# A transformer block with a fast-weight layer and a mixture of experts: the set-up reordered, and the narrow products placed on column groups of the array

## The chip, the cores and the metric

The program runs on one core of one Trainium2 chip. Its time is device microseconds (us) for one execution. Five engines run side by side and meet through semaphores: TensorE (PE, the 128x128 matrix array, whose weight loads are listed as PEld), VectorE (DVE), ScalarE (ACT), GpSimd (POOL) and SyncE (SP), which here only issues transfers. Each engine works through its own list strictly in the order written. In the profile a line such as L1412 is line 1412 of the kernel before.

## What is computed

The input `x` is 2048 rows of 512. One vector `c` gives six modulation rows of 512 (`mod = silu(c) @ wmod`, called here row 0 to row 5): shift, scale and gate for the attention half (0, 1, 2) and for the expert half (3, 4, 5).

```
h = layernorm(x) * (1 + row1) + row0
x = x + gate(row2) * fast_weight_layer(h)
h = layernorm(x) * (1 + row4) + row3
x = x + gate(row5) * experts(h)
```

The fast-weight layer has 4 heads of width 128 and walks over 16 chunks of 128 tokens. For each chunk it makes q, k, v (`silu(h @ W_qkv)`, q and k normalised) and 12 learning rates per token (`softplus(h @ W_lr + b_lr)`). It computes gradients for three 128x128 weight matrices per head, passes each through two Newton-Schulz steps in bf16, adds it to the matrix, rescales the columns, and applies the new matrices to q. The next chunk starts from the new matrices, so the 16 chunks are a recurrence. The expert half sends each token to 2 of 8 experts by router logits `h @ (gate_weight.T + 2 * lora)` and adds low-rank terms to the expert weights.

## The kernel before, in words

**Set-up.** All of it stands ahead of the chunk loop in each engine's list. SP issues `c`, rows 1 and 0 of `wmod`, `W_qkv` in four parts by contraction index, row 2, `W_proj`, rows 4, 3, 5 and two chunks of `x`. ACT issues fifteen more transfers (two chunks of `x`, the three fast-weight matrices, `W_lr`, `b_lr`, the router's and the low-rank factors) and only then runs `silu(c)` (L1333), since the transfers stand first in its list. PE makes rows 1 and 0 as columns (L294, L300: 16 products each of one column), turns the three matrices (`turned`, L112), prepares chunk 0 (L322 to L345: twelve products of 512 columns for q, k, v, and four of 12 columns for the rates, L330), and has the other rows between them: row 2 as a broadcast (L340, cbc, with `c` spread over 128 columns), row 4 as columns (L350), row 3 (L360), row 5 (L366). The low-rank term of the first three expert weight tiles (L394, "mg") closes it. From rows 2 and 5 DVE makes the gates (L770 to L778 and L805 to L812).

**Chunk loop.** One iteration `c` interleaves four strands by an order that is written out for each engine: the fast-weight step of chunk `c` (FWD, N0, N1, N2), the preparation of chunk `c+1` (PREP and RATE), the output of chunk `c-1` (APPLY: products with q, projection, layernorm, router logits, ranks, scatter by an indirect transfer from POOL), and three expert weight tiles (MG: L592 adds the low-rank term, DVE scales it, SP stores it in DRAM). The `heads` helper (L106) runs four products of 128 columns, `turned` (L112) four transposes. The rates are four accumulating products of 12 columns (L474) into `P0[:, 0:12]`, the logits four of 8 columns (L578) into `A0[:, 0:8]`. ACT's `sg` (L1412), the first silu of the fast-weight step, marks each chunk once.

**Tail and experts.** After the loop comes the output of chunk 15, a table of expert blocks, and 39 blocks of expert work (L660, L673). The expert weights are read back into the space of the loop's buffers: five experts when iteration 15 begins, three when its updates have been read.

## Time and profile before

| what | value |
|---|---|
| median of 3 runs | 1042.41 us (1042.32 to 1044.21) |
| the profiled execution | 1043.71 us, span 1042.0 us |
| mean granted TensorE clock | 0.945 |
| busy, share of the span | PE 87%, DVE 63%, ACT 61%, POOL 31% |
| chain that ended last | PE 56%, DVE 20%, ACT 12%, issue 5%, POOL 3% |

### The profile page before, as it was taken

How to read it: one execution, taken by the hardware profiler on the slowest of the kernel's cores; microseconds unless marked ns; L12 is line 12 of the kernel's file. 1: busy time of each engine (PE TensorE's matmuls, PEld its weight loads, DVE VectorE, ACT ScalarE, POOL GpSimd, SP SyncE). 2: the span in 40 equal slices, each digit the busy share in tenths (PEclk: the TensorE clock that was granted, in tenths of full speed). 3: DMA queues.
4: the chain of work that ended last, by engine and by line, in shares of the span. 5: the costliest groups of instructions: out<-in, count | busy, mean ns of one | idle time of the engine just before them, and what ended most of it. 6: DMA issues, size and time to landing. Idle time of an engine off the chain costs nothing.

```text
span 1042.0 us, 16297 instructions
## 1 busy us (share of the span) xinstructions
PE 907.1 (87%) x5123; PEld 575.7 (55%) x5123; DVE 654.5 (63%) x2293; ACT 635.7 (61%) x1378; POOL 320.6 (31%) x283
## 2 busy tenths in 40 slices
PE   1798799999999999999999999986539999999995
PEld 1665476577576576575665765764324444444442
DVE  1145889988889889889789899796332222222221
ACT  0114888888888889788888888886113333333331
POOL 0111333433343443343434344332201222222222
PEclk9978999998999999999999999996659999999998
DMA  9603154364362551561652542439523444444430
GB/s 345 227 1 108 35 143 125 80 163 112 92 163 77 127 163 57 137 162 32 163 136 69 162 126 69 133 90 367 211 71 71 75 81 82 78 78 72 82 55 0
DMA packets 58084, 120.43 MB, mean 116 GB/s; under 512 B 6912, under 2 KB 8576, under 8 KB 56976
## 3 DMA queue, kind: packets, MB, share of 16 engines
q1 hardware_dynamic: 45968, 100.23, 32.6%
q0 software_dynamic: 8176, 16.85, 9.9%
q10 hardware_dynamic: 3856, 2.31, 0.7%
q8 instruction: 42, 0.69, 0.3%
q14 instruction: 42, 0.34, 0.1%
HBM read 51.94 MB, written 69.27 MB: 116 GB/s over the span
## 4 chain that ended last, share of the span: by engine, by line
PE 56%; DVE 20%; ACT 12%; issue 5%; POOL 3%; ACTq 2%; DMA 1%; SPq 0%; POOLq 0%; DVEq 0%
PE bank L660 14%; PE bank L106 11%; PE bank L112 7%; PE bank L673 6%; DVE t_small L993 1%; ACT t_arena L1502 1%; PE bank L494 1%; PE bank L480 1%; PE bank L487 1%; PE bank L474 1%; PE bank L464 1%; POOL t_small L1711 1%; POOL xs_scratch L1722 1%; PE bank L456 1%; PE bank L459 1%
## 5 line engine op out<-in xcount | busy, mean ns | idle before, releaser
L106 PEld LDWEIGHTS bank<-t_arena 128*128 128x128 bf16 (+1 forms) x1536 | 120.1, 123 | 99.7 <-ACT t_arena L1518 18.0
L660 PE MATMUL bank<-t_arena 128*128 x312 | 145.8, 610 | 18.9 <-issue 15.0
L106 PE MATMUL bank<-t_arena 128*128 128x128 bf16 (+1 forms) x1536 | 148.5, 237 | 14.4 <-ACT t_arena L1518 5.3
L1748 POOL DMA_INDIRECT out_x<-t_arena,t_tokx x39 | 60.6, 1553 | 208.3 <-DVE t_small L1302 196.9
L112 PE MATMUL bank<-t_ident,t_arena 128*128 128x128 f32 x618 | 97.5, 281 | 22.7 <-DMA t_arena<-xs_scratch 8.3
L112 PEld LDWEIGHTS bank<-t_ident,t_arena 128*128 128x128 f32 x618 | 75.7, 146 | 74.6 <-issue 43.5
L1307 DVE TENSOR_TENSOR t_arena<-t_arena,bank 128x256 f32<-128x256 f32 x39 | 16.4, 422 | 144.8 <-ACT t_arena L1636 144.8
L1636 ACT ACTIVATE t_arena<-bank 128x256 f32<-128x256 f32 x39 | 15.0, 384 | 148.6 <-PE bank L660 148.6
L660 PEld LDWEIGHTS bank<-t_arena 128*128 128x128 f32 x312 | 56.7, 192 | 85.1 <-issue 85.1
L673 PE MATMUL bank<-t_arena 128*128 x156 | 73.5, 593 | 0.5 <-ACT t_arena L1631 0.5
L1643 ACT ACTIVATE t_arena<-bank,t_small 128x128 f32<-128x128 f32 x156 | 58.7, 456 | 16.5 <-PE bank L112 14.5
L1703 POOL TENSOR_TENSOR t_small<-t_small,t_half 128x8 f32<-128x8 f32 x15 | 26.9, 1794 | 115.9 <-DVE t_small L993 115.9
L1313 DVE SCALAR_TENSOR_TENSOR t_arena<-bank,t_small,t_gbb 128x512 f32<-128x512 f32 x39 | 29.3, 751 | 51.7 <-PE bank L673 47.7
L106 PE MATMUL bank<-t_W,t_arena 128*128 128x128 f32 x384 | 55.1, 299 | 1.5 <-DVE t_arena L1181 1.5
L106 PEld LDWEIGHTS bank<-t_W,t_arena 128*128 128x128 f32 x384 | 51.5, 213 | 3.2 <-DVE t_arena L1181 1.7
L112 PEld LDWEIGHTS bank<-t_identb,t_arena 128*128 128x128 bf16 x384 | 27.6, 99 | 39.4 <-issue 18.5
L1722 POOL DMA_INDIRECT xs_scratch<-t_arena,t_posu x30 | 30.3, 1010 | 45.0 <-DVE t_cum L1175 40.4
L112 PE MATMUL bank<-t_identb,t_arena 128*128 128x128 bf16 x384 | 38.0, 222 | 2.7 <-DVE t_arena L878 0.9
L1697 POOL TENSOR_TENSOR t_small<-t_euler,t_small 128x12 f32<-128x12 f32 x15 | 38.3, 2555 | 0.0
L673 PEld LDWEIGHTS bank<-t_arena 128*128 128x128 f32 x156 | 26.7, 190 | 19.9 <-issue 19.9
L112 PE MATMUL bank<-t_ident,t_WT 128*128 128x128 f32 x192 | 35.4, 334 | 0.9 <-DVE t_WT L1141 0.5
L592 PE MATMUL bank<-t_arena 32*128 32x512 f32 x90 | 19.3, 714 | 16.1 <-ACT t_arena L1563 16.1
(489 smaller groups left out, 2220.6 us busy)
## 6 DMA issues: line engine op xcount, KB each, us to landing
xs_scratch<-t_zero SPq DMA_DIRECT2D x16, 2064.0 KB, 15.0
wm_scratch<-t_arena SPq DMA_DIRECT2D x48, 256.0 KB
t_arena<-wm_scratch SPq DMA_DIRECT2D x8, 1536.0 KB, 18.6
t_arena<-xs_scratch SPq DMA_DIRECT2D x39, 258.0 KB, 2.7
t_arena<-in_gate_up SPq DMA_DIRECT2D x32, 256.0 KB, 12.1
t_arena<-in_wmod SPq DMA_DIRECT2D x6, 1024.0 KB, 17.8
out_x<-t_arena SPq DMA_DIRECT2D x16, 256.0 KB, 2.0
t_arena<-in_down SPq DMA_DIRECT2D x16, 256.0 KB, 12.4
```

Of the source, the lines that this page charges most:

```text
L106: mm = pe.matmul(bank[:, s], lhs[:, s], rhs[:, s], start=True, stop=True)
L112: mm = pe.transpose(bank[:, 128 * k:128 * k + 128], src[:, 128 * k:128 * k + 128], idn)
L592: mm = pe.matmul([P0, P1, P2][j][:, :], la[e % 2][q, 128 * k:128 * k + 128], lb[k // 4][q, :], start=True, stop=True)
L660: mm = pe.matmul(AA[u % 2][:, :], xT[u % 2][:, 128 * k:128 * k + 128], w_e[:, bass.ds(which[u], 1), 512 * k:512 * k + 512], start=(k == 0) ...
L673: mm = pe.matmul(BB[b % 2][:, :], fT[b % 2][:, 128 * k:128 * k + 128], w_e[:, bass.ds(which[b], 1), 2048 + 512 * k:2560 + 512 * k], start= ...
L1307: dve.tensor_tensor(fs[u % 2], ft[u % 2], AA[u % 2][:, 256:512], ALU.mult).then_inc(up_dve, 1)
L1313: dve.scalar_tensor_tensor(out=yb[b % 3], in0=BB[b % 2][:, :], scalar=wx[b % RING], in1=gab[1][:, :], op0=ALU.mult, op1=ALU.mult).then_inc ...
L1643: row = act.activation(xT[t % 2][:, s], P0[:, s], ACT.Identity, scale=cb_c[:, k:k + 1], bias=sb_c[:, k:k + 1])
L1697: pool.tensor_tensor(e12, euler[:, 0:12], na12, ALU.pow).then_inc(rate_pool, 1)
L1703: pool.tensor_tensor(n8, n8, half[:, 0:8], ALU.pow).then_inc(prep_pool, 1)
L1722: pool.indirect_dma_start(out=xs, out_offset=bass.IndirectOffsetOnAxis(ap=posu[a % 2][:, k:k + 1], axis=0), in_=h2x, in_offset=None).then_ ...
L1748: pool.indirect_dma_start(out=out, out_offset=bass.IndirectOffsetOnAxis(ap=tokx[b % RING], axis=0), in_=yb[b % 3], in_offset=None, bounds_ ...
```

## The change

**Transfers.** ACT issues only chunk 0 of `x`. Everything else is issued by SP, in the order of need: `c`, rows 1 and 0, the k third of `W_qkv` (now split by output, with a semaphore each), matrices 2 and 0, `W_lr`, the q third, matrix 1, `b_lr`, the v third, chunk 1 of `x`, the low-rank factors, row 2, `W_proj`, and the rest.

**Rows.** A row is made in two steps. Four products, one for each quarter of the contraction, run with 32 columns of `c` repeated (`cb32`) as weights, each on its own group of 32 array columns, and leave four partial rows in four groups of 32 partitions. ACT copies the bank; a product with a selection matrix (`sel4`, ones in partitions 0, 32, 64, 96) adds the quarters, into columns for rows 0, 1, 3, 4 or as a broadcast for rows 2 and 5. Only rows 1 and 0 stay in the set-up; rows 2, 4, 3 and 5, the gates, the scaling of `W_proj`, the router's merged matrix and the masked low-rank factors move into iteration 0.

**Rates and logits.** `wlr` and `gwm` are padded to 32 columns and become the weights; `hT` and `h2T` stream. Four products of 128 columns on four column groups, a copy of 128x128 by ACT (`lrT`, `lgT`), and one product with `selr` adds the quarters and turns them back.

**Expert tiles.** Four staging buffers instead of two, the low-rank product of tile set `c` in iteration `c` instead of one earlier (iteration 15 has one, the set-up none), other tiles in each set, and the first five experts' tiles finished by set 14.

**Order.** The lists of the loop are written out anew on every engine: `gq` ahead of `hq`, `hbs` ahead of `sg`, the rank product behind the three turns of the new matrices, the stores of tiles at the end of an iteration, and many Newton-Schulz steps exchanged among the three matrices.

```diff
 # PE, set-up
-            for k in range(4):
-                for j in range(4):
-                    mm = pe.matmul(A0[:, k:k + 1], wm[1][:, 512 * j + 128 * k:512 * j + 128 * k + 128], tcol[:, j:j + 1],
-                                   start=(j == 0), stop=(j == 3))
+            pe.wait_ge(set_dve, nth(SET_DVE, 0, "cb32"))
+            for j in range(4):
+                q = slice(32 * j, 32 * j + 32)
+                mm = pe.matmul(A0[q, :], cb32[:, q], wm[1][:, 512 * j:512 * j + 512], start=True, stop=True)
...
+            pe.wait_ge(set_act, nth(SET_ACT, 0, "v1"))
             for k in range(4):
+                mm = pe.matmul(A0[:, k:k + 1], rowp[1][:, 128 * k:128 * k + 128], sel4[:, 0:1], start=True, stop=True)
...
 # PE, rates, in the set-up and in each iteration
                 for k in range(4):
-                    mm = pe.matmul(P0[:, 0:12], hT[p % 2][:, 128 * k:128 * k + 128], wlr[:, k, :], start=(k == 0), stop=(k == 3))
+                    q = slice(32 * k, 32 * k + 32)
+                    mm = pe.matmul(P0[q, 0:128], wlr[:, k, :], hT[p % 2][:, 128 * k:128 * k + 128], start=True, stop=True)
                 mm.then_inc(rate_pe, 1)
...
+                pe.wait_ge(rate_act, nth(RATE_ACT, p, "lrT"))
+                pe.matmul(P0[:, 0:12], lrT[:, :], selr[:, 0:12], start=True, stop=True).then_inc(rate_pe, 1)
...
 # PE, logits (gwm with h2T, lgT) likewise; iteration 0 takes the other rows
+                if c == 0:
+                    pe.wait_ge(s_wm[2],16)
+                    pe.wait_ge(set_dve, nth(SET_DVE, 0, "ca"))
+                    for j in range(4):
+                        q = slice(32 * j, 32 * j + 32)
+                        mm = pe.matmul(A0[q, :], cb32[:, q], wm[2][:, 512 * j:512 * j + 512], start=True, stop=True)
+                    mm.then_inc(mod_pe, 1)
...
 # ACT
-            for c in range(2):
-                act.dma_start(x1[:, c, :], A["x"][128 * c:128 * c + 128, :]).then_inc(s_x[c], 16)
-            for i in range(3):
-                act.dma_start(h4(W[i][:, :]), A[f"w{i}"].rearrange("h p n -> p h n")).then_inc(s_w[i], 16)
-            act.dma_start(wlr[:, :, :], A["W_lr"].rearrange("(k p) n -> p k n", p=128)).then_inc(s_lr, 16)
-            act.dma_start(blr[:, :], A["b_lr"].to_broadcast([128, 12])).then_inc(s_blr, 16)
...
+            act.dma_start(x1[:, 0, :], A["x"][0:128, :]).then_inc(s_x[0], 16)
...
+                act.wait_ge(rate_pe, nth(RATE_PE, p, "lr"))
+                act.copy(lrT[:, :], P0[:, 0:128]).then_inc(rate_act, 1)
...
 # SP
+            row(1)
+            row(0)
+            proj(1)
+            fast(2)
+            fast(0)
+            sp.wait_ge(set_pool, nth(SET_POOL, 0, "wl0"))
+            sp.dma_start(wlr[:, :, 0:12], A["W_lr"].rearrange("(k p) n -> p k n", p=128)).then_inc(s_lr, 16)
+            proj(0)
+            fast(1)
+            sp.dma_start(blr[:, :], A["b_lr"].to_broadcast([128, 12])).then_inc(s_blr, 16)
+            proj(2)
...
+                    sp.wait_ge(s_ms, 48 * (NC - 1))
+                    for n in range(2):
+                        sp.wait_ge(s_z[n], 8 * NC)
                     for e in range(5):
                         expert(e)
...
+                store_tiles(c)
+                if c + 4 < NC:
+                    load_tiles(c + 4)
+            sp.wait_ge(s_ms, 48 * NC)
```

## Rows read from the trace of the kernel before

**Rows 1.** Windows by stage: length; busy (count) PE, PEld, DVE, ACT, POOL; PEclk; DMA; GB/s
```profile
0.00:23.10 23.10, 0.00 (x0) 0.03 (x1) 2.80 (x20) 1.49 (x2) 2.00 (x17) 1.00 0.94 354
23.10:51.00 27.90, 21.39 (x85) 18.53 (x86) 4.70 (x14) 4.93 (x10) 3.64 (x4) 1.00 0.68 241
51.00:66.00 15.00, 15.00 (x63) 9.26 (x62) 8.97 (x26) 2.25 (x3) 3.92 (x2) 0.96 0.01 2
66.00:81.80 15.80, 15.80 (x45) 10.73 (x46) 2.33 (x7) 0.60 (x1) 0.00 (x0) 0.50 0.00 0
81.80:93.10 11.30, 8.41 (x47) 5.94 (x46) 7.39 (x16) 5.06 (x15) 0.00 (x0) 0.85 0.01 2
93.10:132.20 39.10, 31.77 (x218) 20.68 (x218) 31.03 (x96) 30.71 (x63) 11.61 (x9) 0.96 0.31 95
132.20:695.40 563.20, 532.33 (x3727) 366.06 (x3727) 492.93 (x1735) 473.14 (x995) 222.02 (x194) 0.98 0.43 116
695.40:774.70 79.30, 43.98 (x251) 32.36 (x249) 42.49 (x159) 30.95 (x60) 16.84 (x18) 0.68 0.67 236
774.70:1042.00 267.30, 238.41 (x698) 112.10 (x698) 61.83 (x226) 86.61 (x230) 60.58 (x39) 0.98 0.39 67
```

**Rows 2.** Line L1412, the silu that marks each chunk: durations in ns, first and last start
```profile
L1412 ACT ACTIVATE t_arena<-bank x16: 597/597/598, 93.1 to 695.4; 128x512 f32<-128x512 f32 x16
```

**Rows 3.** Chain that ended last, set-up: start us, us, what
```profile
6.33 5.69 ACTq L1322
...
23.10 6.96 PE bank L294 x32
...
43.86 0.56 DVE t_arena L736
44.46 1.13 PE bank L112 x4
45.62 1.51 ACT t_arena L1352 x4
...
49.25 1.71 PE bank L325 x2
...
57.10 3.43 PE bank L340 x8
```

**Rows 4.** Timeline, set-up: the norm of q and k for chunk 0
```profile
57.82 1.06 ACT L1362 ACTIVATE t_arena<-t_arena 128x1024 f32<-128x1024 f32 x1
...
58.91 1.22 DVE L768 TENSOR_REDUCE t_small<-t_arena 128x8 f32<-128x1024 f32 x1 [0.90 <-ACT t_arena L1362]
...
60.21 1.64 POOL L1682 TENSOR_TENSOR t_small<-t_small,t_half 128x8 f32<-128x8 f32 x1 [4.73 <-DVE t_small L768]
```

**Rows 5.** Transfers, 0 to 112 us: rate in 40 equal slices; a transfer, KB, us to landing
```profile
GB/s 40 371 381 413 415 416 401 387 280 368 402 408 401 181 301 156 0 0 6 0 0 0 0 3 0 0 0 0 0 0 3 0 0 281 105 274 273 303 86 6
...
t_small<-in_c SPq DMA_DIRECT2D x1, 2.0 KB, 3.2
```

**Rows 6.** Row groups at work: window of L592 alone (PE, PEld), and the timeline of another
```profile
126.50:128.50 2.00, 1.13 (x6) 0.34 (x6) 1.00 0.00 0
...
368.19 1.86 PE L592 MATMUL bank<-t_arena 32*128 32x512 f32 x6 [1.08 <-ACT t_arena L1563]
369.98 0.19 PE L598 MATMUL bank<-t_msk,t_upperb 128*128 128x8 bf16 x1
```

**Rows 7.** Lines of the rates and a small ACT operation: ns min/median/max, first and last start
```profile
L474 PE MATMUL bank<-t_wlr,t_arena x120: 259/259/259, 103.1 to 667.2; 128*128 128x12 f32 x120
...
L1537 ACT ACTIVATE t_arena<-bank,t_small x60: 449/465/473, 161.7 to 727.3; 128x128 f32<-128x128 f32 x60
```

**Rows 8.** Waits, PE, 132.2 to 695.4 us: total, times, longest
```profile
PE bank L592 <- ACT t_arena L1563: 15.2, 14, 1.1
```

**Rows 9.** Chain that ended last, 340 to 370 us: the rate products of one iteration
```profile
344.61 0.90 PE bank L474 x8
```

**Rows 10.** Timeline of SP: the last three expert loads
```profile
727.73 1.27 SPq L1781 DMA_DIRECT2D t_arena<-wm_scratch  x3
```

More of the change, by code:

```diff
@@ L175, in adaln_block @@
         kl0_0, kl2_0, vl_0, kT_0 = cut(10240, 512, 4)
-        stage = [cut(12288, 512, 3), cut(13824, 512, 3)]
-        wm = cut(12288, 2048, 6)
+        stage = [cut(39428 + 1536 * i, 512, 3) for i in range(4)]
         tg, hb, sg, hid, dgt, pp, dgb, dhm = cut(15360, 512, 8)
@@ new lines, in _ @@
+            pe.wait_ge(set_act, nth(SET_ACT, 0, "v0"))
+            for k in range(4):
+                mm = pe.matmul(A1[:, k:k + 1], rowp[0][:, 128 * k:128 * k + 128], sel4[:, 0:1], start=True, stop=True)
+            mm.then_inc(set_pe, 1)
+            pe.wait_ge(s_w[2],16)
+            pe.wait_ge(set_pool, nth(SET_POOL, 0, "id"))
+            turned(pe, B2, W[2], 4, ident[:, :]).then_inc(set_pe, 1)
+            pe.wait_ge(s_w[0],16)
+            turned(pe, B0, W[0], 4, ident[:, :]).then_inc(set_pe, 1)
@@ L707, in _ @@
-            dve.tensor_scalar(mo[:, :], pcol[:, :], 0.0625, None, ALU.mult).then_inc(set_dve, 1)
-            dve.wait_ge(set_dve, nth(SET_DVE, 0, "mo"))
-            dve.tensor_scalar(me[:, :], mo[:, :], -1.0, 1.0, ALU.mult, ALU.add).then_inc(set_dve, 1)
-            dve.wait_ge(set_act, nth(SET_ACT, 0, "tc"))
-            for k in range(4):
-                row = dve.tensor_scalar(cbc[:, 128 * k:128 * k + 128], ones[:, :], tcol[:, k:k + 1], None, ALU.mult)
-            row.then_inc(set_dve, 1)
@@ L732, in _ @@
                 dve.tensor_scalar(rstd[p % 2], mv[p % 2][:, 1:2], LNEPS, None, ALU.add).then_inc(prep_dve, 1)
+            dve.wait_ge(set_act, nth(SET_ACT, 0, "tc"))
+            for j in range(4):
+                ins = dve.tensor_scalar(cb32[:, 32 * j:32 * j + 32], ones[:, 0:32], tcol[:, j:j + 1], None, ALU.mult)
+            ins.then_inc(set_dve, 1)
+            if p < NC:
                 dve.wait_ge(prep_pool, nth(PREP_POOL, p, "rs"))
@@ L1377, in _ @@
                     act.wait_ge(apply_pe, nth(APPLY_PE, p-2, "hq"))
[L1378 to L1379 removed]
                 act.copy(qT[p % 2], P0[:, :]).then_inc(prep_act, 1)
                 act.wait_ge(rate_dve, nth(RATE_DVE, p, "lr"))
+                act.wait_ge(prep_dve, nth(PREP_DVE, p, "tk"))
+                if p >= 2:
+                    act.wait_ge(n0_pe, nth(N0_PE, p-2, "G"))
+                for h in range(H):
+                    s = slice(128 * h, 128 * h + 128)
+                    row = act.activation(kl0[p % 2][:, s], raw[1][:, s], ACT.Identity, scale=lr12[p % 2][:, 0 + h:1 + h])
+                row.then_inc(prep_act, 1)
                 act.wait_ge(prep_act, nth(PREP_ACT, p, "raw2"))
@@ L1397, in _ @@
                 row.then_inc(prep_act, 1)
-                if p >= 2:
-                    act.wait_ge(n0_pe, nth(N0_PE, p-2, "G"))
-                for h in range(H):
-                    s = slice(128 * h, 128 * h + 128)
-                    row = act.activation(kl0[p % 2][:, s], raw[1][:, s], ACT.Identity, scale=lr12[p % 2][:, 0 + h:1 + h])
-                row.then_inc(prep_act, 1)
             for c in range(NC):
@@ L1586, in _ @@
                     act.wait_ge(n0_pe, nth(N0_PE, c, "TW"))
-                    if c >= 1:
-                        act.wait_ge(apply_pe, nth(APPLY_PE, c-1, "gq"))
                     act.copy(W[0][:, :], B0[:, :]).then_inc(n0_act, 1)
+                if p < NC:
+                    if p >= 2:
+                        act.wait_ge(n2_pe, nth(N2_PE, p-2, "G"))
+                    for h in range(H):
+                        s = slice(128 * h, 128 * h + 128)
+                        row = act.activation(kl2[p % 2][:, s], raw[1][:, s], ACT.Identity, scale=lr12[p % 2][:, 8 + h:9 + h])
+                    row.then_inc(prep_act, 1)
+                if 0 <= c < NC:
                     act.wait_ge(n1_pe, nth(N1_PE, c, "TW"))
@@ L1593, in _ @@
                     act.copy(W[1][:, :], B1[:, :]).then_inc(n1_act, 1)
-                if p < NC:
-                    if p >= 2:
-                        act.wait_ge(n0_pe, nth(N0_PE, p-2, "G"))
-                    for h in range(H):
-                        s = slice(128 * h, 128 * h + 128)
-                        row = act.activation(kl0[p % 2][:, s], raw[1][:, s], ACT.Identity, scale=lr12[p % 2][:, 0 + h:1 + h])
-                    row.then_inc(prep_act, 1)
             a = NC - 1
```

1294 lines of the change are left out of this document (689 added, 605 removed).

## The prediction

> **What bounds the kernel now.** The windows by stage come first [rows 1]. Up to 93.1 us is set-up, then 16 chunks to about 738, a tail, and from 774.7 the expert blocks. Three things are to be seen. In the first 23 us PE does nothing, although the DMA engines are 0.94 busy. From 132 to 695 PE is busy 532.33 of 563.20 us, 94.5%, against 88% for DVE and 84% for ACT: TensorE bounds the loop, the two others are close behind. The marker of the chunks confirms the pace: 15 steps from 93.1 to 695.4, 40.15 us each [rows 2]. Third, the granted clock: the stretch 66 to 81.8 runs at 0.50 with PE never idle.
>
> The chain of the set-up says why it is 93 us long [rows 3]. ACT is still issuing transfers (the one for `b_lr` alone holds it for 5.69 us), so `silu(c)` and with it L294 start at 23.1. The data was not the cause: transfers run at some 400 GB/s from the third microsecond, and `c` lands 3.2 us after its issue [rows 5]. Then the products of one column: 32 instructions in 6.96 us, 0.218 each, twice over. The clock column reads 1.00 there, but a 512-column product took 1.71 us at 49 us and 0.86 us at 57 (8 instructions in 3.43 us), so PE ran at its lower level, 1.2 GHz, through 51 us. After 57, PE works for rows 2 to 5, which chunk 0 doesn't need, in front of chunk 0's last turns.
>
> **The set-up, step by step, to the marker.** Removed: ACT's fourteen transfers ahead of `silu(c)`, both one-column row products, rows 2 to 5, the router's matrix, the masks and the first tile product. What is left is a chain of latencies.
> 1. `x` and `c` are issued at 0.8 us and land near 4 to 4.5 [rows 5]. Normalising and the short handshakes end in L736's operation (0.56) at about 7. PE turns chunk 0 while row 1 arrives (1 MB, 2.6 us at 400 GB/s): 1.13 us [rows 3], 8.2.
> 2. Rows 1 and 0 on column groups. The trace has no column group, but the tile products L592 have row groups: their three products of 512 columns run together, 1.13 us in all at full clock, where one after the other would be 6 x 0.43 = 2.6; 1.86 us at half clock [rows 6]. Bounds for four column groups: 1.86 each if they run together, 6.9 (8 x 0.86) if not, at half clock. I take 1.86, since the row groups show it: 12.
> 3. Adding the quarters: 8 instructions of one column at 0.218, twice, 3.5: 15.5. Shift and scale of the turned rows, 1.51 [rows 3], plus a short DVE step: 17.2.
> 4. Rates 0.8 at half clock, the first k product 1.71, the selection 0.4, then seven q and k products at 0.86, the first of them perhaps at 1.71: 27.3. Full clock came after 4 us of 512-column work before; here the dense work begins at 15.5 with the turns of two matrices.
> 5. Silu 0.6 [rows 2], square 1.06, sum 1.22, power 1.64 [rows 4], four small DVE steps and one turn, about 2: 34.
> 6. ACT, in its order: three copies at 0.6, three groups of four scalings near 1.3 (by L1352's 1.51), the copy `hbs` 0.6: the marker at about 40.5.
>
> So it moves from 93.1 to 40.5: -52.6 us. Data for it is 5.8 MB, 14.5 us at 400 GB/s, a cover for steps 1 to 4. SP now carries `W_lr` and `b_lr`, and the q third, matrix 1, the v third and all later ones queue behind them. With 3 and 5.7 us of issue [rows 3] and half a microsecond for each other, the v third leaves at 14 and lands near 20, against a need at 27. If backlog added 8 us to that, the cover is gone. Bounds of the set-up: 36 (full clock from step 4, quick issue) to 50.
>
> **Iteration 0** takes on PE four row products at 1.13, two broadcasts at 0.86, two column forms of 8 instructions near 1, and the router's four small ones, 0.6: 8.8 us. It has no APPLY, which is why PE is busy only 31.77 of its 39.1 us [rows 1]. The room is 7.3, so I add 1.2 us; the bounds are 0 and 3. DVE's gates and scalings, some twenty operations, take the place of APPLY's. SP loads four tile sets only behind these products, but the tiles are first needed at its end, over 20 us later.
>
> **Rates and logits.** Old: 8 instructions, 0.90 us on the chain [rows 9]; each lasts 259 ns while one is issued every 120 [rows 7]. New: two passes of 128 columns, 0.21, and a tail of at most 1.13 - 0.86 = 0.27, which the next product may hide; then two instructions of selection, 0.24. That is 0.45 to 0.72 against 0.90 to 0.96, a gain of 0.2 to 0.5; I take 0.3, for two such blocks per chunk 0.6. ACT gets two copies of 128x128, under 0.45 each [rows 7], and is 84% busy. Both round trips have other products written between their halves. Over 15 steps: -9 us. The tile product waits 1.1 us per chunk for ACT's last turn copy [rows 8]; it is the largest wait, and it stays, with `lgT` now ahead of that copy.
>
> The Trainium skill (TensorEngine Tiling (Array Packing), Key Properties) says that changing the tiling mode drains TensorE. By it each chunk would pay four more switches. The trace has one entry and one exit per chunk, at L592, and L598 is recorded 0.07 us before L592's last end [rows 6], which does not look like a long drain.
>
> **The new order of the loop** has no price in any row. The rank product leaves the path of the three turns (0.3 gained), `gq` ahead of `hq` starts APPLY's silu earlier; `lgT` is late. Against 2.2 us of PE idle per step (30.9 over 14), nothing larger than -1.5 or +1.5 per step is at hand; I take 0 and keep both. **Tail:** iteration 15 now holds a tile product, in a stretch where PE is idle half the time [rows 1]; the last expert loads, issued at 727.7 [rows 10] for work at 774.7, may go 20 us later. Logits at half clock are 0.4 shorter. Expert blocks are unchanged.
>
> **Sum.** -52.6 + 1.2 - 9 - 0.4 = -60.8; span 1042.0 to 981.2. The profiled execution lies 1.7 above its span and 1.3 above the median of the runs: 981.6, told as 982.
>
> **The rivals.**
> - *The gain of the narrow products is eaten.* Four changes of tiling per chunk at the full tail of 0.27 are 1.1 us, against at most 1.0 gained. The loop stays at 40.15: 991. For it: nothing in rows has a column group between full products. This is also what the skill's rule would make of it.
> - *The loop gets longer.* PE waits at a selection product for ACT, which works in order behind bf16 copies of 0.6 us; two such waits of 0.4 to 0.5 per step, net +1 against now: 982 + 9 + 15 = 1006.
> - *The loop gets shorter by the order too.* Half of the 2.2 us idle goes, in addition: 982 - 15 = 967.
> - *The set-up stays bound by issue or clock.* SP's narrow transfers hold the thirds of `W_qkv` back 8 us, or q, k, v run at 1.2 GHz (seven products, +6): 990.
> - *The column groups run one after another,* so the change does not do what it says: two row products +5 each in the set-up, four at +2.3 in iteration 0, each block of four 0.86 + 0.24, 0.15 longer than before, so +0.45 against my term, 0.9 per step: 982 + 10 + 9 + 13 = 1014.
> - *Slower than before.* The only place large enough is the loop: the new lists must cost 61 / 16 = 3.8 us per step more than I have, for instance each selection product stalling PE 1.9 us behind ACT's and DVE's copies for Newton-Schulz. DVE and ACT at 88% and 84% would have to be reordered badly; at 4.5 per step it is 1054.
>
> **How the numbers follow.** My case 0.42, eaten gain 0.17, longer loop 0.12, shorter loop 0.17, held set-up 0.06, groups in turn 0.04, slower 0.02. The likeliest gives 982; its own range is 975 to 989. For 8 in 10 the range takes in the held set-up, the eaten gain, most of the shorter loop and a part of the longer: 966 to 1001. This kernel's runs tell 0.2%, 2 us, from no change. Every case but the last is far below 1040: faster 0.97, same 0.01, slower 0.02.
>
> **What would show it.** The marker L1412's successor first at 36 to 46 us, last some 593 later (15 steps of 39.5). Row products of four at once, near 1.9 us for the first two. The rate block near 0.5 on PE, and its selection without a wait. PE over 94% busy in the loop. No PE wait on a `W_qkv` third. It is wrong if the steps are over 40.5 or under 38.5, or if the first marker is beyond 50.

## The result and the profile after

| kernel | median us | against before, 95% interval |
|---|---|---|
| changed (4 runs, 1002.8 to 1007.9) | 1006.4 | 0.9642 [0.9613, 0.9671] |
| the same again, beside the experiments (6 runs, 999.5 to 1004.7) | 1001.6 | 0.9609 [0.9584, 0.9634] |

It is faster by 3.6 to 3.9%, where 5.8% was forecast. 1006 lies above the range of 966 to 1001, and the median of the repeat, 1001.6, still just above it. The profiled execution took 1002.8 us with a span of 1001.1.

The windows by stage of the changed kernel (columns as in [rows 1]) say where the 20 us between forecast and measurement went:

```profile
0.00:37.50 37.50, 27.59 (x126) 14.64 (x126) 13.03 (x60) 15.88 (x35) 9.76 (x25) 0.91 1.00 348
37.50:85.90 48.40, 39.29 (x264) 25.10 (x265) 41.45 (x119) 33.24 (x70) 12.81 (x9) 0.93 0.58 166
85.90:528.90 443.00, 412.64 (x2971) 271.43 (x2970) 392.74 (x1364) 377.25 (x803) 194.72 (x152) 1.00 0.39 117
528.90:653.80 124.90, 117.05 (x812) 78.11 (x812) 107.58 (x373) 103.68 (x221) 53.58 (x42) 0.97 0.33 98
653.80:733.80 80.00, 46.83 (x261) 31.19 (x261) 44.44 (x159) 31.29 (x62) 18.42 (x18) 0.68 0.57 218
733.80:1001.10 267.30, 238.53 (x698) 112.10 (x698) 61.79 (x226) 86.61 (x230) 60.56 (x39) 0.98 0.38 67
```

The marker, now line L1478:

```profile
L1478 ACT ACTIVATE t_arena<-bank x16: 597/603/617, 37.5 to 653.8; 128x512 f32<-128x512 f32 x16
```

| part | before | after | difference | forecast |
|---|---|---|---|---|
| set-up, to the first marker | 93.1 | 37.5 | -55.6 | -52.6 |
| iteration 0 | 39.1 | 48.4 | +9.3 | +1.2 |
| iterations 1 to 14 | 563.2 | 567.9 | +4.7 | -8.4 |
| last marker to the experts | 79.3 | 80.0 | +0.7 | -0.4 |
| expert blocks | 267.3 | 267.3 | 0 | 0 |

(The forecast for iterations 1 to 14 is 14 of its 15 blocks at 0.6; the fifteenth stands in no row.) The set-up is right; iteration 0 and the steps are not. From marker to marker the 15 steps take 41.1 us on average, over the 40.5 at which the prediction called itself wrong.

The steps have to be read with the granted clock beside them. A stretch in which it falls to its lower level, 0.5, is called a drop below, and a step without one a full-clock step. Below are single steps from marker to marker: first iteration 5 of the changed kernel, as nine in a row are (40.3 us), then iteration 12.

```profile
247.01:287.28 40.27, 37.58 (x272) 24.69 (x272) 35.76 (x125) 34.31 (x75) 17.89 (x14) 1.00 0.39 119
528.95:571.15 42.20, 39.61 (x272) 26.63 (x272) 36.42 (x125) 34.73 (x74) 17.99 (x15) 0.96 0.39 116
```

Before, a step without a stretch of half clock took 39.3 us (132.2 to 171.5, for one), but 8 of the 14 were longer, up to 42.0, seven of them with such a stretch: 13.0 us in all above 14 x 39.3. So two things changed at once. The full-clock step is 1.0 us *longer*, and from iteration 1 to 528 us no step has a drop. Over the eleven steps of iterations 1 to 11 the two cancel: 443.3 us before (132.2 to 575.5), 443.1 after (85.9 to 529.0). What is left of the +4.7 lies in the last three.

### The profile page after: what moved, and what is told of

Read it like the earlier page. It is cut to its first block, busy times and chain, and to the rows that moved or that the text cites. A ratio compares the mean times of both kernels' runs of the same rounds, so it can differ in the third digit from the quotient of the medians.

```text
span 1001.1 us, 16358 instructions
## 1 busy us (share of the span) xinstructions
PE 881.9 (88%) x5127; PEld 532.6 (53%) x5127; DVE 661.0 (66%) x2299; ACT 647.9 (65%) x1416; POOL 349.8 (35%) x285
## 4 chain that ended last, share of the span: by engine, by line
PE 59%; DVE 16%; DMA 7%; POOL 7%; issue 6%; ACT 4%; SPq 0%; POOLq 0%; DVEq 0%; ACTq 0%
PE bank L714 15%; PE bank L110 11%; PE bank L116 8%; PE bank L727 7%; DMA xs_scratch<-t_arena 5%; POOL xs_scratch L1814 2%; POOL t_small L1801 2%; PE bank L487 1%; PE bank L549 1%; PE bank L498 1%; PE bank L559 1%; PE bank L503 1%; PE bank L529 1%; PE bank L467 1%; PE bank L536 1%
## 5 line engine op out<-in xcount | busy, mean ns | idle before, releaser
L110 PEld LDWEIGHTS bank<-t_arena 128*128 128x128 bf16 (+1 forms) x1536 | 123.5, 122 | 83.6 <-issue 15.9
L110 PE MATMUL bank<-t_arena 128*128 128x128 bf16 (+1 forms) x1536 | 152.7, 236 | 8.7 <-DVE t_arena L860 2.3
L116 PE MATMUL bank<-t_ident,t_arena 128*128 128x128 f32 x618 | 102.6, 285 | 41.5 <-DMA t_arena<-xs_scratch 8.4
L116 PEld LDWEIGHTS bank<-t_ident,t_arena 128*128 128x128 f32 x618 | 72.4, 143 | 98.7 <-issue 40.4
L110 PEld LDWEIGHTS bank<-t_W,t_arena 128*128 128x128 f32 x384 | 47.9, 201 | 5.5 <-DVE t_arena L886 4.5
L116 PEld LDWEIGHTS bank<-t_identb,t_arena 128*128 128x128 bf16 x384 | 27.3, 102 | 42.1 <-issue 14.7
L1801 POOL TENSOR_TENSOR t_small<-t_small,t_half 128x4 f32<-128x4 f32 x16 | 30.6, 1915 | 54.1 <-DVE t_small L1130 54.1
L727 PEld LDWEIGHTS bank<-t_arena 128*128 128x128 f32 x156 | 26.7, 190 | 19.9 <-issue 19.9
L1793 POOL TENSOR_TENSOR t_small<-t_euler,t_small 128x12 f32<-128x12 f32 x15 | 35.5, 2364 | 0.4 <-DVE t_small L945 0.4
L642 PE MATMUL bank<-t_arena 32*128 32x512 f32 x96 | 23.4, 662 | 13.4 <-ACT t_arena L1648 13.4
```

The lines of the kernel that those rows point to most:

```text
L110: mm = pe.matmul(bank[:, s], lhs[:, s], rhs[:, s], start=True, stop=True)
L116: mm = pe.transpose(bank[:, 128 * k:128 * k + 128], src[:, 128 * k:128 * k + 128], idn)
L642: mm = pe.matmul([P0, P1, P2][j][:, :], la[e % 2][q, 128 * k:128 * k + 128], lb[k // 4][q, :], start=True, stop=True)
L727: mm = pe.matmul(BB[b % 2][:, :], fT[b % 2][:, 128 * k:128 * k + 128], w_e[:, bass.ds(which[b], 1), 2048 + 512 * k:2560 + 512 * k], start= ...
L1793: pool.tensor_tensor(e12, euler[:, 0:12], na12, ALU.pow).then_inc(rate_pool, 1)
L1801: pool.tensor_tensor(wss[2], wss[2], half[:, 0:4], ALU.pow).then_inc(n2_pool, 1)
```

## The set-up on the chip

The timeline of PE in the changed kernel: start us, us, what, idle before it in brackets.

```profile
6.15 1.12 PE L116 MATMUL bank<-t_ident,t_arena 128*128 128x128 f32 x4 [6.15 <-DVE t_arena L770]
7.19 1.94 PE L318 MATMUL bank<-t_arena 128*32 128x512 f32 x8
9.37 1.52 PE L323 MATMUL bank<-t_arena 128*32 128x512 f32 x8 [0.24 <-DMA t_arena<-in_wmod]
10.83 1.05 PE L327 MATMUL bank<-t_arena 128*128 128x1 f32 x8
11.74 1.03 PE L331 MATMUL bank<-t_arena 128*128 128x1 f32 x8
...
15.10 0.66 PE L344 MATMUL bank<-t_arena,t_wlr 128*32 128x128 f32 x8
15.69 2.08 PE L348 MATMUL bank<-t_arena 128*128 128x512 f32 x2
...
19.69 1.48 PE L356 MATMUL bank<-t_arena 128*128 128x512 f32 x2
21.00 1.02 PE L357 MATMUL bank<-t_arena 128*128 128x512 f32 x2
```

Four column groups do run together: a row's eight instructions of 512 columns take 1.94 us (1.86 was taken from the row groups). L348 at 2.08 shows the lower level, 1.2 GHz; L357 at 1.02 the upper, 2.4 GHz, from about 20 us on. For L318 the level is read from durations too, since the clock column has 1.00 there: the same block takes 1.06 in iteration 0 (L523, below). The eight one-column instructions take 1.0, not 1.74, which is 1.5 of the 3 us that the set-up is better. The remainder was not followed step by step.

## Experiments

All are edits of the changed kernel unless said otherwise. Set-up and iteration 0 vary by 1 to 2 us between the profiled executions (first marker at 37.5 and 36.0 in two of the changed kernel, up to 37.9 in the edits with both products narrow), so the steps are compared by the trace, marker to marker.

### Order or narrow products

`wide_again`: rates and logits as before, all else as changed.

```diff
-                        q = slice(32 * k, 32 * k + 32)
-                        mm = pe.matmul(P0[q, 0:128], wlr[:, k, :], hT[p % 2][:, 128 * k:128 * k + 128], start=True, stop=True)
+                        mm = pe.matmul(P0[:, 0:12], hT[p % 2][:, 128 * k:128 * k + 128], wlr[:, k, 0:12], start=(k == 0), stop=(k == 3))
...
-                    pe.wait_ge(rate_act, nth(RATE_ACT, p, "lrT"))
...
-                    pe.matmul(P0[:, 0:12], lrT[:, :], selr[:, 0:12], start=True, stop=True).then_inc(rate_pe, 1)
```

> The changed kernel, nothing edited. It is the base for the three others, and says how far its time moves from run to run: its four runs so far lie between 1002.8 and 1007.9 us, those of the kernel before within 1042.3 to 1044.2. Both theories expect 1003 to 1008 us and a step of 40.2 to 40.3 us at full clock.

> The changed kernel with the rates and the logits as the four accumulating 12- and 8-column products of before; no quarters, no ACT copy of them, no selection product. Set-up, iteration 0 and the order of all the rest stay as changed. A step of the changed kernel takes 40.2 to 40.3 us where a full-clock step of before took 39.3. Theory A (the order of the loop's lists, with which PE stands idle 2.7 us a step instead of 2.2 and issues other stalls, is what costs): the step stays at 40.2 us or rises by the 1.0 us of longer product blocks to 41.2, total 1006 to 1020 us. Theory B (the two round trips PE to ACT to PE of the narrow products stall PE): the step falls to about 39.3 us, total about 991 us.

`narrow_before`: the kernel before, with the narrow products, their copies, padding and selection matrix alone.

```diff
+                    act.wait_ge(rate_pe, nth(RATE_PE, p, "lr"))
...
+                    act.copy(lrT[:, :], P0[:, 0:128]).then_inc(rate_act, 1)
+                if 0 <= c < NC:
                     act.wait_ge(n2_pe, nth(N2_PE, c, "A0"))
```

> The kernel before with the narrow products alone: rates and logits as four products on column groups, an ACT copy of their quarters and the selection product, with the zero padding and the selection matrix made in set-up; order of everything else, set-up and tile sets as before. Theory A (the new order of the lists costs, the narrow products gain what they shorten PE's blocks by): a full-clock step falls from 39.3 to 38.6 us, total about 1043 - 15 x 0.6 = 1034 us. Theory B (the round trips cost more than the blocks give): a full-clock step rises to about 40.2 us, total about 1055 us.

The unedited kernel took 1001.6 us, 1.4 under what was expected of it, with the same full-clock step of 40.27. `wide_again` took 1014.8 us (0.9726 [0.9702, 0.9750]), as Theory A has it. `narrow_before` took 1069.1 us (1.0239 [1.0213, 1.0265]), 14 more than its Theory B, the worse one. A full-clock step and one with a drop in `wide_again`, then a typical step of `narrow_before`:

```profile
86.81:127.06 40.25, 37.91 (x268) 25.66 (x267) 35.14 (x124) 33.95 (x72) 15.78 (x12) 1.00 0.37 104
168.11:209.86 41.75, 39.52 (x268) 27.34 (x268) 36.07 (x125) 34.42 (x73) 17.88 (x14) 0.96 0.38 115
```

```profile
263.09:304.38 41.29, 38.02 (x272) 25.75 (x271) 35.23 (x124) 34.47 (x73) 15.75 (x15) 0.96 0.42 114
```

With the wide products back, the full-clock step stays at 40.2: the 1.0 us is the order's, and the narrow products take nothing off a full-clock step. Yet the 14 steps take 583.4 instead of 567.9 us. Nearly all of that is clock: seven of them have drops. 8.2 of the 15.4 us lie in iterations 12 to 14, where the tile sets share row groups (next section); over iterations 1 to 11 the difference is 7.3. And in the old order the narrow products *cost*: not one step of `narrow_before` is free of a drop, 584.1 us for 14.

Where the clock falls: windows around one drop in `wide_again` (204.8), then around one in `narrow_before` (172.6), and that kernel's PE timeline ahead of it.

```profile
198.00:204.80 6.80, 5.18 (x30) 2.82 (x29) 6.34 (x24) 6.07 (x16) 4.27 (x4) 1.00 1.03 285
204.80:208.20 3.40, 3.40 (x18) 3.34 (x19) 2.65 (x12) 3.09 (x10) 0.71 (x1) 0.51 0.37 113
```

```profile
166.00:172.60 6.60, 4.47 (x39) 2.97 (x38) 6.26 (x22) 6.34 (x16) 3.10 (x3) 1.00 0.13 41
172.60:176.30 3.70, 3.70 (x20) 2.50 (x15) 3.70 (x16) 2.81 (x9) 0.83 (x2) 0.54 0.01 2
```

```profile
168.81 0.42 PE L598 MATMUL bank<-t_arena,t_gwm 128*32 128x128 f32 x8 [0.35 <-ACT t_arena L1573]
...
172.22 1.66 PE L616 MATMUL bank<-t_arena 32*128 32x512 f32 x6 [1.56 <-ACT t_arena L1604]
```

In iterations 1 to 14 of these kernels it always falls in the same place: the end of a step, where PE does logits, three turns with waits, stands idle for ACT's last copy, and runs the tile products. PE is then never idle for the 3.4 to 3.7 us of half clock, so each drop costs about half of them, 1.5 to 1.8 us. In `narrow_before`, with ACT's extra copy ahead, that idle time is 1.56 us where it was 1.08 [rows 6].

### Tile sets

`tiles_apart`: the same 48 tiles, given to the sets so that only set 15 has two tiles of one row group.

```diff
-    out = [[left[0].pop(0), left[1].pop(0), left[2 + m % 2].pop(0)] for m in range(12)]
-    return out + [[left[2 + (m + j) % 2].pop(0) for j in range(3)] for m in range(4)]
...
+    for m in range(15):
+        skip = (3, 2, 3, 2, 3, 0, 1, 3, 2, 0, 1, 3, 2, 0, 1)[m]
+        out.append([left[q].pop(0) for q in range(4) if q != skip])
+    return out + [[left[3].pop(0), left[2].pop(0), left[3].pop(0)]]
```

> The changed kernel with another assignment of the 48 expert tiles to the 16 sets, so that three tiles of a set lie in three different row groups in sets 0 to 14 (in the changed kernel sets 12 to 15 hold two tiles of one group); only set 15 keeps two of one group. In the profile the tile products of sets 12 to 14 take 1.95 us instead of 1.13 and the steps 42.3, 41.8 and 40.8 us instead of 40.2, and a stretch of half clock follows. Theory A (the shared group is the cause of the longer last steps): the steps 12 to 14 fall to 40.3 us each, total 3 to 5 us below the changed kernel. Theory B (something else at the end of the loop lengthens them, or the half-clock stretches fall elsewhere): less than 1.5 us below.

997.8 us (997.4 to 998.8; 0.9570 [0.9547, 0.9593]), 3.8 below the changed kernel beside it: Theory A. Iteration 12, for the 42.20 above, and the tile products at the drop of the changed kernel (PE's timeline):

```profile
527.46:567.73 40.27, 37.58 (x272) 24.69 (x272) 35.78 (x125) 34.30 (x74) 17.89 (x14) 1.00 0.42 119
```

```profile
564.16 1.95 PE L642 MATMUL bank<-t_arena 32*128 32x512 f32 x6 [0.88 <-ACT t_arena L1648]
566.04 2.21 PE L116 MATMUL bank<-t_ident,t_WT 128*128 128x128 f32 x12
```

Two tiles in one row group run one after the other, 1.95 us instead of 1.13, and the half clock follows. All 14 steps without it: 563.9 us, 0.7 from the 563.2 of before. So nearly all of the loop's +4.7 is the tile sets, and the new order and the narrow products together come out at about nothing. The five executions lie within 1.4 us of each other; those of `data_later`, with the same sets, spread over 6.1, so a smaller variation is not shown.

### Iteration 0, POOL's order, the set-up's data, the rates alone

These four start from `tiles_apart`. `iter0_light`: zeroing and masks to DVE's gap in the set-up; row 5's gate to the tail.

```diff
                 if c == 0:
...
-                    dve.memset(zero, 0.0).then_inc(mod_dve, 1)
...
-                    dve.wait_ge(mod_pe, nth(MOD_PE, 0, "b5"))
-                    dve.tensor_scalar(gbb[:, :], A1[:, :], 0.0, 2.0, ALU.is_ge, ALU.mult).then_inc(mod_dve, 1)
...
+                    act.copy(gbb[:, :], A1[:, :]).then_inc(mod_act, 1)
```

> On top of the version with the tile sets apart (997.8 us, iteration 0 46.8 us): the zeroing of the scatter's clear buffer and the two mask products of the adapters go from iteration 0 to the end of DVE's set-up list, where DVE is idle 4.2 us (three operations, 1.6 us), and row 5's gate (five DVE operations, 3.2 us between 76.1 and 79.3, ahead of the scaling of WT[2]) goes to the tail, with one ACT copy of the row (0.6 us) in its place. Theory A (iteration 0 is bound by DVE working its list in order, so the row gates that my sum hid in the missing APPLY are on the path): iteration 0 falls by 4 to 5 us, to about 42.5, total about 993.5 us. Theory B (PE's added products, 39.3 us busy in it, or the half clock bind): it falls by less than 1 us. The tail may get up to 3 us longer under both if the gate is late there.

992.7 us, 5.1 less, but iteration 0 itself only 46.8 to 45.0, between the two theories (43.3 in `best_all` below, with the clock at 1.00). The rest is a first marker at 36.0 instead of 37.6, which is within what executions differ, and some 2 us behind the last marker, so that the total agrees with Theory A by luck.

Where PE waits longest for DVE in iteration 0, in the changed kernel, the first at its start (for whom, us in total, times, longest):

```profile
PE bank L110 <- DVE t_arena L860: 2.3, 1, 2.3
PE bank L485 <- DVE t_small L928: 1.8, 1, 1.8
PE bank L116 <- DVE t_WT L1178: 1.5, 1, 1.5
```

L928 stands in DVE's list behind row 2's gate, and L1178 behind row 5's, five operations of 3.1 us each (46.5 to 49.7 us and 76.1 to 79.3). The kernel before waits at neither place in iteration 0. The one for L1178 is gone in `iter0_light`, where the gate has left; the one for L928 is 1.6 there.

`rs_first`:

```diff
+                if c + 2 < NC:
+                    pool.wait_ge(prep_dve, nth(PREP_DVE, c + 2, "ve"))
+                    pool.tensor_tensor(rstd[c % 2], rstd[c % 2], mhalf[:, 0:1], ALU.pow).then_inc(prep_pool, 1)
                 if a >= 0:
                     pool.wait_ge(s_z[a % 2],16 * (a // 2 + 1))
```

> On top of the version with the tile sets apart (997.8 us, steps of 40.3 us): on POOL the power for the next chunk's normalisation goes ahead of the two scatters that it stood behind, and on DVE the two small operations that it needs go right behind the statistics. The chain of each step runs scatter, scatter, power, then DVE's hA, behind which the sums for matrix 2 and the operand of PE's next product stand; DVE is idle 0.48 us for it. Theory A (this wait is on the path that sets the step): steps fall by 0.5 us or more, to 39.8 or less, total 990 us or less. Theory B (the rest of the step has the room, and the step is set by another chain): steps stay at 40.2 to 40.3, total 997 to 999 us.

993.2 us, between the two theories. Steps of 40.0 instead of 40.3, 559.6 us for 14: 0.3 a step, less than DVE's 0.48 us of idle time that went, so the wait was on the path in part.

```profile
243.69:283.66 39.97, 37.27 (x272) 24.65 (x272) 36.01 (x125) 34.24 (x74) 17.64 (x14) 1.00 0.45 119
```

`data_later`, in SP's list:

```diff
+            row(2)
             proj(2)
```

> On top of the version with the tile sets apart (997.8 us, first marker at 37.6 us): SP issues row 2 of the modulation (1 MB) ahead of the third of W_qkv for v instead of behind it. It tests the cover that the prediction gave the set-up's data: Theory A (the data of steps 1 to 4 lands well before its use): the marker stays within 0.5 us of 37.6, total unchanged. Theory B (the set-up runs at the pace of its data): the v third comes 2.6 us later and the marker with it, at 40.2, total about 1000.4 us.

The marker stays at 37.6, the total at 998.9 (994.3 to 1000.4), and PE waits for no third of `W_qkv`: Theory A. Another 1 MB ahead of the v third costs nothing.

`rates_wide`: the edit of `wide_again`, for the rates alone.

> On top of the version with the tile sets apart (997.8 us; steps of 40.3, no clock drop in the loop): the rates alone go back to four accumulating 12-column products, with no copy and no selection; the logits stay narrow. With both wide the same order had a stretch of half clock in every second or third step, each after the logits, the turns, 0.9 us of idle and the tile products. Theory A (what keeps the clock is the shorter sparse stretch at the step's end, so the narrow logits do it): the clock stays at 1.00, steps 40.2 to 40.4 us, total within 1 us of 997.8. Theory B (both narrow blocks count, being work of few columns wherever they stand): drops come back, each some 1.6 us, total 1003 to 1009 us.

1001.8 us, 4.0 more, with the clock at 1.00 in every step. Theory A is right on the clock: with narrow logits there is no drop. It is wrong on the length: each step is 0.34 longer, close to the 0.3 that the narrow rates were sized at. (Both wide gave 40.2: the two blocks' effects don't add up, each holds beside the other only.)

```profile
247.29:287.90 40.61, 37.91 (x270) 25.20 (x270) 35.68 (x125) 34.20 (x73) 17.89 (x14) 1.00 0.43 118
```

### The three gains together, and three edits on top

> The three edits that gained, together: tile sets apart, the light iteration 0, POOL's power ahead of the scatters. If they add, as separate stages should: 997.8 - 5.1 - 4.6 = 988 us, steps of 40.0, iteration 0 at 45 to 46 us. If they overlap (iteration 0 already takes the power's gain), 989 to 991 us.

989.9 us (0.9478 [0.9446, 0.9509]), steps of 40.0 and iteration 0 at 43.3, below the 45 to 46 expected, with no drop in it: the fastest kernel of this study, ahead of both kernels.

`logits_wide`: the edit of `wide_again`, for the logits alone.

> All three edits, and the logits alone as four accumulating 8-column products again, with no ACT copy and no selection; the rates stay narrow. Measured so far with the changed order: both wide 40.2 us a step, only the logits narrow 40.6, both narrow 40.3. So narrow rates give 0.3 and narrow logits should cost 0.3 to 0.4 (PE waits for DVE right behind them, so a shorter block is only a longer wait, while ACT's copy and the selection stand ahead of the turns). Theory A (that sum holds): full-clock steps fall from 40.0 to 39.6 us; in the first steps and as far as the clock stays at 1.00, total 982 to 984 us. Theory B (the 8-column products at the step's end bring the half clock back, as with both wide): every second or third step 1.5 us longer, total 988 to 994 us. Theory C (the narrow logits cost nothing): steps stay at 40.0.

998.1 us: Theory C for the step (39.97 us, the same), Theory B for the clock: five of 14 steps have a drop. The narrow logits give nothing but the clock, 6.6 us over the loop.

```profile
201.28:241.25 39.97, 37.63 (x270) 25.21 (x270) 35.98 (x125) 34.03 (x74) 17.64 (x14) 1.00 0.41 120
241.25:282.35 41.10, 38.86 (x270) 26.79 (x270) 36.29 (x125) 34.45 (x73) 17.64 (x14) 0.96 0.40 117
```

`k_first` moves two DVE operations one place forward each.

```diff
+                    dve.tensor_tensor(h4(raw[1]), h4(raw[1]), bc(r8[:, 4:8]), ALU.mult).then_inc(prep_dve, 1)
...
                     dve.tensor_reduce(wss[2], h4(sq3[2]), AX, ALU.add).then_inc(n2_dve, 1)
...
-                    dve.tensor_tensor(h4(raw[1]), h4(raw[1]), bc(r8[:, 4:8]), ALU.mult).then_inc(prep_dve, 1)
```

> All three edits, and on DVE the scalings of k and q, for which PE's turns wait 0.6 and 0.2 us a step, go one operation further forward each: k ahead of the sum for matrix 2, q ahead of the sum for matrix 0. It tests what in the new order costs the 0.9 us a step by which its full-clock step (both products wide) is over that of before. Theory A (the turns at the step's end wait in DVE's list, DVE being busy without a gap for 9 us there): steps fall by 0.4 to 0.6 us to 39.4 to 39.6, total 980 to 982 us. Theory B (the three sums and scalings of the matrices are as urgent, and the wait moves to the turns of WT): steps within 0.15 us of 40.0.

1004.4 us: the full-clock steps are 39.9, as Theory B has it, but half of the steps now have drops, 574.0 us for 14. PE's waits in it (for whom, us in total, times, longest), 200 to 640 us: two short waits for DVE have become one of 1.0 for ACT.

```profile
PE bank L119 <- ACT t_arena L1637: 9.6, 10, 1.0
PE bank L645 <- ACT t_arena L1651: 9.3, 10, 0.9
```

`g2_late`: row 2's gate and W_proj's scaling behind the last tile operation of iteration 0 in DVE's list.

```diff
-                    dve.tensor_scalar(ga, A0[:, :], 0.0, 2.0, ALU.is_ge, ALU.mult).then_inc(mod_dve, 1)
...
+                    act.copy(ga, A0[:, :]).then_inc(mod_act, 1)
```

> All three edits, and row 2's gate (five DVE operations, 3.1 us from 44 us on) and the scaling of W_proj by it (2.7 us from 51.7) go from the middle of iteration 0 to its end on DVE's list, where DVE is idle 2.7 us for PE; one ACT copy of the row takes their place. Taking 5.2 us of other DVE work out of iteration 0 gave only 1.8 us. Theory A (what is on DVE ahead of the Newton-Schulz operands is what counts, and these 5.8 us are that): iteration 0 with iteration 1 falls by 2.5 to 4 us, total 984 to 986 us. Theory B (PE's added products, 7.5 us, and their clock are what is left): less than 1 us.

994.9 us: worse, which neither theory has. PE's wait behind row 2's gate is gone from iteration 0, but it has a drop there, and early in iteration 1 PE is idle for 3.3 us in one piece, with a drop behind it. Iterations 0 and 1 take 44.2 and 45.8 us with the clock at 0.92 and 0.93, against 43.3 and 40.0.

### The old lists under the new set-up

These three start from `tiles_apart` with the light iteration 0; from iteration 1 on PE, DVE, ACT and POOL work their lists of before. SP keeps its new one, and the tile products their new iteration. The cut shows the loop of one engine.

```diff
-            for c in range(NC):
+            for c in range(1):
...
+            for c in range(1, NC):
```

> The changed kernel's set-up, with the tile sets apart and the light iteration 0 (992.7 us, steps of 40.3 us with the new lists and both narrow products); from iteration 1 on every engine works the lists of the kernel before (the tile products stay in the iteration of the changed kernel), and rates and logits are the accumulating 12- and 8-column products. Theory A (the order of the lists alone makes the full-clock step 0.9 us longer): full-clock steps of 39.3 to 39.4 us, with the half-clock stretches of before at about every second step, 1.3 to 2 us each; 14 steps in 561 to 566 us, total 990 to 995 us. Theory B (something else of the new kernel does it: the later place of the tile products, SP's issue order, buffers): full-clock steps of 40.2 us.

> As the kernel with the lists of before, and the rates alone as four products on column groups with their copy and selection; the logits keep the accumulating 8-column products. In the new order narrow rates, beside narrow logits, took 0.34 us off a step. Theory A (the rates stand in the stretch where PE works without a wait, the logits where PE waits for ACT): full-clock steps of 39.0 us, total 3 to 5 us below the one with both wide. Theory B (narrow products cost in this order wherever they are): full-clock steps of 39.3 or more.

> As the two others, with both products narrow. The kernel before with both narrow took 41.3 us a step, every one with a half-clock stretch, PE waiting 1.56 us ahead of the tile products instead of 1.08. Theory A (the logits' copy and selection push ACT's last copies and lengthen that wait, whatever the set-up): steps of 41.3 us with the clock at 0.96 in each, total 18 to 22 us above the one with both wide or with only the rates narrow. Theory B (it was peculiar to that kernel's tile order or set-up): steps of 39.3 to 40.3.

997.6, 1004.6 and 1015.0 us. Neighbouring steps of `old_wide`, then of `old_rates_narrow`:

```profile
285.77:325.08 39.31, 37.15 (x268) 25.39 (x267) 34.24 (x121) 33.76 (x71) 15.54 (x14) 1.00 0.38 115
325.08:365.81 40.73, 38.57 (x268) 26.30 (x267) 36.30 (x129) 33.89 (x71) 16.03 (x15) 0.96 0.38 120
```

```profile
326.83:366.91 40.08, 37.06 (x270) 24.95 (x269) 34.23 (x121) 34.11 (x73) 15.73 (x14) 1.00 0.39 113
366.91:407.55 40.64, 37.32 (x270) 24.93 (x269) 35.33 (x126) 34.28 (x72) 16.03 (x14) 1.00 0.39 118
```

`old_wide` has the steps of Theory A: 39.3 us, 563.7 for 14 steps (the total is 2.6 over its range). The lists of the four engines are the whole 1.0 us; SP's issue order, the buffers and the place of the tile products, all still new here, are not. In `old_rates_narrow` Theory A falls: the rates cost 0.8 to 1.3 in the steps shown, although only four of 14 have a drop and eight have in `old_wide`. `old_lists` has the steps of its Theory A, 41.4 us and each with a drop, at 17.4 us above `old_wide`: the drops of `narrow_before` do not hang on its set-up. The timelines of `old_rates_narrow`, DVE and then PE, show how the rates cost; the last line is the same DVE operation in `old_wide`:

```profile
339.21 0.17 DVE L1518 TENSOR_TENSOR t_small<-bank,t_blr 128x12 f32<-128x12 f32 x1 [1.20 <-PE bank L753]
...
339.50 0.69 DVE L1527 TENSOR_TENSOR t_arena<-t_arena,t_small 128x512 bf16<-128x512 bf16 x1
```

```profile
338.88 0.29 PE L753 MATMUL bank<-t_selr,t_lrT 128*128 128x12 f32 x2
339.02 0.38 PE L134 MATMUL bank<-t_arena 128*128 128x128 bf16 x4
340.24 0.40 PE L140 MATMUL bank<-t_identb,t_arena 128*128 128x128 bf16 x4 [0.84 <-DVE t_arena L1527]
```

```profile
297.25 0.17 DVE L1505 TENSOR_TENSOR t_small<-bank,t_blr 128x12 f32<-128x12 f32 x1 [0.29 <-PE bank L734]
```

L753 is the selection product of the rates. DVE stands 1.20 us for it, where it stood 0.29 for the wide one, with the operand of the next Newton-Schulz step (L1527) behind it in the list, and PE then stands 0.84 us for that. The narrow product is shorter and its result *later*, by a copy and a second product.

All in one table, 14 steps each:

| order | rates | logits | full-clock step | 14 steps | run |
|---|---|---|---|---|---|
| old | wide | wide | 39.3 | 563.2, 563.7 | before, old_wide |
| old | narrow | wide | 40.1 to 40.9 | 572.7 | old_rates_narrow |
| old | narrow | narrow | none free of a drop | 584.1, 586.4 | narrow_before, old_lists |
| new | wide | wide | 40.2 | 583.4 (shared groups in it) | wide_again |
| new | wide | narrow | 40.6 | 568.7 | rates_wide |
| new | narrow | narrow | 40.3 | 567.9; 563.9 tiles apart | changed, tiles_apart |
| new, POOL's power first | narrow | narrow | 40.0 | 559.8 | best_all |
| new, POOL's power first | narrow | wide | 40.0 | 566.4 | logits_wide |

The rows don't add up to one price for the order and one for the narrow products. Taken after the new order, the narrow products give 15.4 us (583.4 to 567.9). In the old order they cost 20.9 (563.2 to 584.1).

## Why the prediction was right in the set-up and wrong behind it

**Set-up, -52.6: right, 3.0 too little.** (Its step 4 adds up to 27.0, not 27.3.) The chain ran as numbered, the groups together, full clock from about 20 us, the q and k products over at 25.5 (forecast 27.3), the marker at 37.5. The cover of the data held (`data_later`).

**Iteration 0, +1.2: wrong, it was +9.3.** The step that failed is "The room is 7.3, so I add 1.2 us". (8.8 - 7.3 is 1.5; the slip is small.) PE's busy time grew by 7.5 us, near the 8.8 costed, but its idle time did not shrink, it grew, from 7.3 to 9.1. The second step that failed is that DVE's operations "take the place of APPLY's", at no cost: PE waits 1.8 and 1.5 us for DVE operations that stand behind the gates of rows 2 and 5, 3.3 of the 9.1. With row 5's gate, the zeroing and the masks moved away, DVE is busy 37.0 instead of 41.2 us and the iteration 1.8 us shorter. The clock has a part as well: 48.3 us at 0.93, 43.3 at 1.00 in `best_all`, where PE is busy 5.2 us more than before and idle 1.0 less. That the rest of the idle time is made of hand-overs on the recurrence, which added products push back, is an argument: no run moved the products alone. The cost of the new order in this iteration was not separated either.

**Rates and logits, -9: the sign of the total is right, the mechanism was not.** The term was the block's time on PE, 0.3 less for each, and that was right: L615's takes 0.43 and its selection L626 0.29, where L578's took 1.06. (The prediction's "one is issued every 120" is not in [rows 7], where x120 is the count; 8 in 0.90 us, [rows 9], are 112 ns.) What failed is that a shorter block is a shorter step: the pair takes nothing off a full-clock step. At the end of a step PE waits for DVE and ACT at once after the logits, so a shorter block is a longer wait. What the pair gives in the new order is clock, 15.4 us over 14 steps and 8.2 of them with shared row groups, a term that the prediction did not have at all. The rival that the gain is eaten came true for the full-clock step, and not for the reason that it gave. Its price was 0.27 us for each change of tiling, and the changes cost less. These are PE's lines in iteration 0 (a row's products) and in iteration 5 (the rate block L472 and its selection L491) of the changed kernel:

```profile
57.51 1.06 PE L523 MATMUL bank<-t_arena 128*32 128x512 f32 x8
58.51 0.40 PE L110 MATMUL bank<-t_arena 128*128 128x128 bf16 x4
...
254.93 1.10 PE L467 MATMUL bank<-t_arena 128*128 128x512 f32 x2
255.97 0.43 PE L472 MATMUL bank<-t_arena,t_wlr 128*32 128x128 f32 x8
...
257.89 1.10 PE L487 MATMUL bank<-t_arena 128*128 128x512 f32 x2
258.83 0.29 PE L491 MATMUL bank<-t_selr,t_lrT 128*128 128x12 f32 x2
```

Coming out costs at most 0.14 us: the next instruction starts 1.00 us after the row's block, where a single product of 512 columns takes 0.86 (L340, [rows 3]). Going in shows 0.10: the product ahead of the rate block takes 1.04 from its start to the block's, the same form ahead of the selection product, which stays on the whole array, 0.94. The Trainium skill (TensorEngine Tiling (Array Packing), Key Properties) has TensorE drain at each change of tiling mode. The traces leave room for a drain of that size and for no longer one.

**Loop order, 0: wrong.** It costs 1.0 us per full-clock step, 13.3 us over 14, shown by `old_wide` and `wide_again`. 1.0 was inside the +-1.5 that I kept, but then cancelled by the centre. With wide products the same order also has 6.9 us more above its full-clock steps than before, nearly all of it drops (583.4 = 14 x 40.25 + 19.9; 563.2 = 14 x 39.3 + 13.0); 12.3 of the 19.9 are in the three steps with shared row groups. 13.3 + 6.9 - 15.4 = +4.8 is the +4.7 of the loop taken apart along one path, and no test of it: the terms hold for that path only. With both products narrow, the new order takes 16.2 us off the 14 steps (584.1 to 567.9).

**Tile sets: overlooked.** "Other tiles in each set" was told in the change and costed at nothing; two tiles share a row group in each of sets 12 to 15, 4.0 us. [Rows 6] was read for what three different groups do, and not asked whether the new sets still had three.

The rival "the loop gets longer" gave 1006, the measured number, and is still not what happened: it has PE waiting at the selection products, where no wait is listed in a full-clock step of the new order, and neither the clock nor iteration 0. That the number agrees is luck.

**Left open.** Which exchange in the lists makes the 1.0 us. Old and new lists of single engines were not mixed, since each waits for the others' order. One piece is found (POOL's power behind the scatters, 0.3 us). Most of the 1.0 is not even recorded as a wait: PE's busy time is 0.76 higher in the new order with the same instructions (37.91 against 37.15 us), its idle time 0.17. Why is not shown. The clock's part is open as well: the runs show after what work it falls, and not what in that work decides it.

## What to carry to other kernels

Idle time of the engine that bounds a recurrent loop is not room by itself (7.3 us of it took in nothing here): count an added operation in full unless it takes a place where its engine waits for something that it does not delay, and look through the other engines' lists for what will stand behind their share of the added work. A product made shorter by splitting it and adding it up elsewhere gives its result later, so ask first who stands in line behind that result, on every engine. And compare steps at the same granted clock before explaining them: here the order made each full-clock step 1.0 us longer while the drops went, and over eleven steps only their sum of nothing shows.

## What the runs showed of the hardware

- In iterations 1 to 14 the clock falls at the end of a step, where PE ran short or few-row products with waits between them. Edits that took next to nothing off a full-clock step decided over 4 to 14 us in this way: narrow logits (steps with a drop: from five to none), tile sets (two to none), two DVE operations moved by one place (none to seven). In `g2_late` a drop stands behind 3.3 us of idle instead.
- Four products of 512 columns and two instructions each, on four column groups of 32, took 1.94 us at the lower clock level, 1.2 GHz, and 1.06 at the upper; four of 128 columns on four groups 0.43 us at the upper. A change to column groups shows 0.10 us, one back at most 0.14. Two tiles in one row group of 32 take turns: 1.95 us for three tiles instead of 1.13.
- Eight one-column instructions took 1.0 us, where 32 of them had taken 0.218 each in the set-up of before [rows 3].
